# Two buffers for the gated output, two banks for the first final block's turns, two logits moved ahead

## The chip, the core and the metric

One core of a Trainium2 chip runs the whole program. The metric is the time of one execution on the device in microseconds; lower is better. TensorE (PE) multiplies, VectorE (DVE), ScalarE (ACT) and GpSimd (POOL) work element by element, and SyncE (SP) issues the DMAs. Each engine takes its instructions in the order of its own queue, and semaphores hold an instruction back until what it needs is there. Matmul results go to PSUM, eight banks of 128 x 512 float32.

## The reference

The input x is 2048 tokens of 512 features. Three layers follow one another:

```python
x = x + 0.5 * ffn(layernorm(x))
x = x + attn(layernorm(x))
x = x + 0.5 * ffn(layernorm(x))
```

`ffn` computes 64 router logits for each token, a softmax, keeps the 8 largest weights, and returns `flat * w_sum + w_dense @ expert_bias`. `attn` is a chunked linear attention with 32 heads (8 groups of 4) of 128 features and chunks of 128 tokens:

```python
scores = q_chunk @ k_chunk.T
decay = where(causal, exp(G[i] - G[j]), 0)
y = (scores * decay) @ xc + (q_chunk * exp(G)) @ prev_state
state = state * chunk_decay + k_dec.T @ xc
y = y / rms(y) * gnorm_w * silu(gate)
out = y.reshape(L, H * D) @ Wo.T
```

## The kernel before

x stays in SBUF as ACC, 16 chunks of 128 tokens. The first expert layer runs in four blocks of four chunks (f = 0 to 3). Then the attention runs over 8 groups g of heads, and in each over 16 steps n, one chunk each; the last expert layer runs in blocks f = 4 to 7 (NB = 4, so NB is the first final block). Products that need float32 accuracy are three bfloat16 products of high and low parts (`mm3`, L323 to L325).

A step n does the following, with the engine in brackets. `scores(n+1)` (PE, bank 2). `read_state(n)` (PE) multiplies the queries with the state into B_IN, bank 5. `attend(n)` (PE) multiplies PH, PL with the values into B_PV, bank 4, and then makes the chunk's state in bank 6; its first part waits for `gated(n-1)`, which reads B_PV. `scale_inter(n)` (DVE, L1649) writes B_IN times a decay to YF, `combine(n)` (DVE, L1656) adds YF into B_PV, `square(n)` (ACT, L1199) writes the squares to YF and their sums to SS, `inv_rms(n)` (POOL, L1453 RM, L1456 RR) takes the inverse root, `gated(n)` (DVE, L1689) writes B_PV times RR times the gate to YF. In the next step `z_hi(n)` (ACT, L1207) and `z_lo(n)` (POOL, L1449) split YF into ZS, a DMA turns it into ZT (`turn_z`), and two steps later `project_out(n)` (PE) multiplies it with Wo and `add_out(n)` (DVE, L1703) adds the product to ACC. Beside these, `decayed(n+1)` (DVE, L1640) waits for the scores, `p_hi(n+1)` (ACT, L1175) and `p_lo(n+1)` (POOL, L1445) split it into PH and PL, which `attend(n)` must have read, `mask_rows(n+2)` (POOL, L1423) prepares the next decay, `update_state(n)` (DVE, L1670), `state_hi(n)` (ACT, L1189) and `state_lo(n)` (DVE, L1678) carry the state on.

The order on each engine is written out by hand, in one `step` function for each engine: L1045 (PE), L1296 (ACT), L1519 (POOL) and L1799 (DVE). In the last group the final expert blocks are woven in. `pe_turn(NB, ...)` transposes chunks of ACC into a bank (L526), and `act_turned` copies the bank to XT (L536). Before, all four turns of block NB go to bank 0, so each waits for the copy of the one before it; the turns 1 and 3 stand between `scores` and `read_state` in the steps 13 and 14, the turns 0 and 2 at the ends of the steps 12 and 13. `pe_logits` (L553) multiplies XT with the router. `dve_logits`, `dve_choose` and `dve_weigh` pick the weights (L564 to L600), `pe_weights` (L617) transposes them, `pe_mix` (L645, L646) multiplies them with the expert biases, and `dve_mixed` (L701) adds the result to ACC. `pool_residual` (L670) scales ACC before.

`project_out` writes to bank 7 (B_OUT) up to n = 11 and to the banks 1 and 3 in turn from n = 12, in the last group. Behind the last step, PE's queue is `project_out(14)`, the weights and the mix of block NB, the logits of block NB + 1 (bank 7), a wait for the mix's last addition, `project_out(15)`, then the blocks NB + 1 to NB + 3. QF holds the rotated queries of a block of four chunks; in the last four steps there is no next block, so nothing is projected (`filled` is empty).

## Time and profile before

| | us |
|---|---|
| median of 3 runs | 1639.38 |
| lowest and highest | 1639.04, 1642.29 |
| profiled execution | 1642.75 |
| its span | 1640.9 |
| PE busy, share | 1589.4, 97% |
| POOL busy, share | 1411.7, 86% |
| DVE busy, share | 1368.9, 83% |
| ACT busy, share | 1093.0, 67% |

The trace is that of the profiled execution, and its times are microseconds from the start of the span. The span is what the core's instructions cover; 1.85 us of the profiled execution lie around it. A busy share is a mean over the whole span; what a change in one stretch is worth has to be read in that stretch. In a timeline row the bracket gives the idle time of the engine just before and what ended it. Operations of one engine overlap a little: the next one starts some 0.1 us before the end that is shown.

### The profile page before, as it was taken

The page shows a single profiled execution, that of the slowest core. Times are in us where ns is not written, and L with a number is a line of the kernel's source. Part 1 is how long each engine was busy: PE and PEld are TensorE (multiplying, and loading weights), DVE is VectorE, ACT ScalarE, POOL GpSimd, SP SyncE. Part 2 cuts the span into 40 slices and gives each one's busy share as a digit, 9 for nine tenths or more (in the row PEclk, how much of TensorE's full clock was granted, in tenths as well). Part 3 has the DMA queues.
Part 4 walks back from the last instruction along what each step waited for, and adds up shares of the span by engine and source line. Part 5 has one row for each costly group of instructions (what it writes and reads, how often), then busy time and mean ns, then how long its engine had stood idle before and what let it go on. Part 6 is the DMA issues. An engine that isn't in the chain of part 4 may idle for free.

```text
span 1640.9 us, 33589 instructions
## 1 busy us (share of the span) xinstructions
PE 1589.4 (97%) x11028; PEld 883.8 (54%) x11028; DVE 1368.9 (83%) x2945; ACT 1093.0 (67%) x2987; POOL 1411.7 (86%) x1316
## 2 busy tenths in 40 slices
PE   7898999999999999999999999999999999999986
PEld 5554555555555555555555555555555555555554
DVE  6988788888878888787878888788888878788876
ACT  4666677676766677766766667666776667666653
POOL 4767899888988899888998989888998889888974
PEclk8999999999999999999999999999999999999998
DMA  5123233232333223231332224323342224322222
GB/s 211 39 55 67 55 74 87 65 72 52 78 85 78 53 59 102 54 83 47 91 78 64 61 64 92 72 72 53 73 95 59 72 46 97 72 65 52 53 45 103
DMA packets 208012, 118.76 MB, mean 72 GB/s; under 512 B 173792, under 2 KB 174816, under 8 KB 206816
## 3 DMA queue, kind: packets, MB, share of 16 engines
q1 hardware_dynamic: 207840, 116.63, 29.7%
q8 instruction: 89, 1.46, 0.4%
q14 instruction: 83, 0.68, 0.1%
HBM read 70.19 MB, written 4.46 MB: 45 GB/s over the span
## 4 chain that ended last, share of the span: by engine, by line
PE 74%; POOL 11%; DVE 8%; issue 4%; ACT 2%; DMA 0%; ACTq 0%; POOLq 0%; DVEq 0%
PE B L325 23%; PE B L323 23%; PE B L324 23%; POOL QS L1410 2%; POOL ROWS L1423 2%; POOL RR L1456 1%; DVE WL L1696 1%; POOL PL L1445 1%; PE B L553 1%; POOL ZS L1449 1%; POOL WVF L1433 1%; POOL K L1417 1%; POOL WVL L1441 1%; POOL RM L1453 1%; DVE PF L1640 1%
## 5 line engine op out<-in xcount | busy, mean ns | idle before, releaser
L323 PE MATMUL B<-WH,XTH 128*128 128x128 bf16 (+1 forms) x992 | 269.3, 296 | 0.6 <-DVE QF L1610 0.6
L324 PE MATMUL B<-WL,XTH 128*128 128x128 bf16 (+1 forms) x992 | 269.3, 296 | 0.0
L325 PE MATMUL B<-WH,XTL 128*128 128x128 bf16 (+1 forms) x992 | 269.3, 296 | 0.0
L1410 POOL TENSOR_TENSOR QS<-QS,SIN 128x512 f32<-128x512 f32 x160 | 219.3, 1371 | 42.8 <-ACT QS L1137 42.7
L323 PE MATMUL B<-XTH,WH 128*128 128x512 bf16 x640 | 243.2, 380 | 1.0 <-DVE G L1630 1.0
L325 PE MATMUL B<-XTH,WL 128*128 128x512 bf16 x640 | 243.3, 380 | 0.0
L324 PE MATMUL B<-XTL,WH 128*128 128x512 bf16 x640 | 243.2, 380 | 0.0
L1689 DVE SCALAR_TENSOR_TENSOR YF<-B,RR,G 128x128 f32<-128x128 f32 x512 | 144.2, 344 | 113.4 <-POOL RR L1456 113.3
L1169 ACT ACTIVATE PF<-ROWS,NG 128x128 f32<-128x128 f32 x512 | 162.7, 389 | 79.1 <-POOL ROWS L1423 78.8
L1449 POOL TENSOR_TENSOR ZS<-YF,ZS 128x512 bf16<-128x512 f32 x128 | 158.0, 1235 | 64.5 <-ACT ZS L1207 64.2
L1136 ACT ACTIVATE QS<-B 64x512 f32<-64x512 f32 x160 | 94.9, 593 | 150.3 <-PE B L325 143.5
L1423 POOL TENSOR_TENSOR ROWS<-ROWS,AFTER 128x512 f32<-128x512 f32 x128 | 189.8, 1483 | 2.4 <-DMA ROWS<-rows_dram 2.4
L323 PE MATMUL B<-WH,ZT 128*128 128x512 bf16 x480 | 181.9, 379 | 0.2 <-DVE ACC L1703 0.2
L324 PE MATMUL B<-WL,ZT 128*128 128x512 bf16 x480 | 181.9, 379 | 0.0
L325 PE MATMUL B<-WH,ZT 128*128 128x512 bf16 x480 | 181.9, 379 | 0.0
L1678 DVE TENSOR_TENSOR STL<-ST,STH 128x512 bf16<-128x512 f32 x120 | 145.1, 1209 | 39.4 <-ACT STH L1189 37.6
L1445 POOL TENSOR_TENSOR PL<-PF,PH 128x512 bf16<-128x512 f32 x128 | 148.1, 1157 | 17.8 <-ACT PH L1175 17.4
L1640 DVE SCALAR_TENSOR_TENSOR PF<-B,DT,PF 128x128 f32<-128x128 f32 x512 | 143.0, 339 | 21.7 <-ACT PF L1169 20.2
L1199 ACT ACTIVATE YF<-B 128x128 f32<-128x128 f32 x512 | 134.0, 276 | 31.1 <-DVE B L1656 28.2
L1615 DVE TENSOR_TENSOR QF<-QF,QS 128x512 f32<-128x512 f32 x128 | 138.0, 1080 | 5.1 <-POOL QS L1410 4.0
L1433 POOL TENSOR_TENSOR WVF<-VF,WJ 128x512 f32<-128x512 f32 x120 | 141.8, 1181 | 0.2
L1456 POOL TENSOR_TENSOR RR<-RM,HALF 128x4 f32<-128x4 f32 x128 | 132.8, 1037 | 10.0
(209 smaller groups left out, 4320.9 us busy)
## 6 DMA issues: line engine op xcount, KB each, us to landing
ROWS<-rows_dram SPq DMA_DIRECT2D x128, 256.0 KB, 3.2
STAGE<-in_wall SPq DMA_DIRECT2D x108, 256.0 KB, 2.8
ACC<-in_x SPq DMA_DIRECT2D x3, 1024.0 KB, 10.0
out<-ACC SPq DMA_DIRECT2D x3, 1024.0 KB, 3.9
ZT<-ZS SPq DMA_TRANSPOSE x128, 3.1
ACC<-in_x SPq DMA_DIRECT2D x4, 256.0 KB, 3.6
COS<-in_cos SPq DMA_DIRECT2D x1, 1024.0 KB, 12.0
SIN<-in_sin SPq DMA_DIRECT2D x1, 1024.0 KB, 14.7
```

The costliest lines, as they stand in the source:

```text
L323: nc.tensor.matmul(out_, ah, bh, start=first, stop=False)
L324: nc.tensor.matmul(out_, ah, bl, start=False, stop=False)
L325: return nc.tensor.matmul(out_, al, bh, start=False, stop=last)
L1169: ins = nc.scalar.activation(PF[:, c], ROWS[:, n % 2, c], ACT.Exp, bias=tab(NG, g, n)[:, h:h + 1], scale=-1.0)
L1410: nc.gpsimd.tensor_tensor(QS[:, sl, :], QS[:, sl, :], SIN[:, t0:t0 + TB], ALU.mult).then_inc(sin_ready.sem, 1)
L1423: nc.gpsimd.tensor_tensor(rows, rows, AFTER[:, None, :].broadcast_to([P, G, P]), ALU.add).then_inc(rows_masked.sem, 1)
L1433: nc.gpsimd.tensor_tensor(WVF[:, :, :], VF[b % 2][:, None, s * P:(s + 1) * P].broadcast_to([P, G, P]), tab(WJ, g, n)[:, :, None].broadcast ...
L1445: nc.gpsimd.tensor_tensor(PL[:, :], PF[:, :], PH[:, :], ALU.subtract).then_inc(pl_ready.sem, 1)
L1449: nc.gpsimd.tensor_tensor(ZS[:, 1, :], YF[:, :], ZS[:, 0, :], ALU.subtract).then_inc(zl_ready.sem, 1)
L1456: nc.gpsimd.tensor_tensor(RR[:, :], RM[:, :], HALF[:, :], ALU.pow).then_inc(rr_ready.sem, 1)
L1640: ins = nc.vector.scalar_tensor_tensor(PF[:, c], B_S[:, c], dt[:, h:h + 1], PF[:, c], ALU.mult, ALU.mult)
L1678: nc.vector.tensor_tensor(STL[:, :], ST[:, :], STH[:, :], ALU.subtract).then_inc(stl_ready.sem, 1)
```

## The change

In the steps 13, 14 and 15 of the last group (`at_end`), the gated output and what becomes it lies in QF[:, 0, :] where n is odd and in YF where n is even (`y_of`). `scale_inter(n)` waits there for the `z_lo` of step n - 2 and, once, for the last readers of QF.

The turns of block NB go to the banks 0 and 7 in turn. The turns 0 and 1 have their banks free without a copy, but turn 1 waits for `add_out(10)`, the last reader of bank 7; turn 2 and turn 3 wait for the copies of the turns 0 and 1. Turn 1 moves behind `read_state(13)`, ahead of `attend(13)`; ScalarE's copy of it moves behind `wv_hi(14)`. `project_out(11)` writes to bank 3.

Behind the last step the logits of block NB + 1 are taken in two halves: chunks 0 and 1 ahead of the expert weights' turn of block NB, chunks 2 and 3 between that turn and the mix. Before, all four stood behind the mix.

```diff
--- before.py
+++ after.py
@@ -190,7 +190,7 @@
         def turned(f, i):
             if f < NB:
                 return t_bank("turn", f, i)
-            return BANK[0] if f == NB else BANK[(2, 6)[i % 2]]
+            return BANK[(0, 7)[i % 2]] if f == NB else BANK[(2, 6)[i % 2]]
 
         def t_bank(kind, f, i):
             return BANK[T_BANK[T_ORDER.index((kind, f, i)) % 3]]
@@ -329,7 +329,15 @@
             return BANK[EARLY_BANK[at]] if at < NFILL else RING[(at - NFILL) % len(RING)]
 
         def out_bank(n, last):
-            return RING[n % 2] if last and n >= NCH - BLK else B_OUT
+            return RING[n % 2] if last and n > NCH - BLK - 2 else B_OUT
+
+        def at_end(g, n):
+
+            return g == KVH - 1 and n > NCH - BLK
+
+        def y_of(g, n):
+
+            return QF[:, 0, :] if at_end(g, n) and n % 2 else YF[:, :]
 
         def tab(T, g, n):
 
@@ -516,8 +524,10 @@
                     pe.wait_ge(out_free.sem, out_free.at(KVH - 1, (f - NB) * BLK + i))
                 if f < NB:
                     t_free(pe, "turn", f, i)
+                elif f == NB and i >= 2:
+                    pe.wait_ge(f_xnt.sem, f_xnt.at(NB, i - 2))
                 elif f == NB and i:
-                    pe.wait_ge(f_xnt.sem, f_xnt.at(NB, i - 1))
+                    pe.wait_ge(out_free.sem, out_free.at(KVH - 1, NCH - BLK - 2))
                 elif f == NB + 1 and i < 2:
                     pe.wait_ge(st_ready.sem, st_ready.at(KVH - 1, cs_event(NCH - 2)))
                 elif f > NB:
@@ -940,7 +950,7 @@
 
 
                 into = out_bank(n, last)
-                if last and n >= NCH - BLK:
+                if last and n > NCH - BLK - 2:
                     pe.wait_ge(ring_free.sem, ring_free.at(g, use_of(NB - 1, NFILL - 1)))
                     pe.wait_ge(out_free.sem, out_free.at(g, n - 2))
                 else:
@@ -1050,13 +1060,15 @@
                         fill(g, b + 1, filled(n, last)[x], n, b == NB - 1, g + 1)
                 if not (last and n == NCH - 1):
                     scores(g, n + 1)
-                if last and n in (NCH - 3, NCH - 2):
-                    pe_turn(pe, NB, (1 if n == NCH - 3 else 3,))
+                if last and n == NCH - 2:
+                    pe_turn(pe, NB, (3,))
                 slot("A")
                 if g == 0 and n in SUMS_STEP:
                     pe.wait_ge(out_free.sem, out_free.at(0, n - 3))
                     pe_sums(pe, SUMS_STEP[n])
                 read_state(g, n)
+                if last and n == NCH - 3:
+                    pe_turn(pe, NB, (1,))
                 if last and n == NCH - 1:
                     pe_turn(pe, NB + 1, (0, 1))
                 if g == 0 and n == 0:
@@ -1090,9 +1102,10 @@
             for n in steps(True):
                 step(KVH - 1, n, True)
             project_out(KVH - 1, NCH - 2, True)
+            pe_logits(pe, NB + 1, (0, 1))
             pe_weights(pe, NB)
+            pe_logits(pe, NB + 1, (2, 3))
             pe_mix(pe, NB)
-            pe_logits(pe, NB + 1)
             pe.wait_ge(f_acc.sem, acc_at(NB, BLK - 1))
             project_out(KVH - 1, NCH - 1, True)
             pe_turn(pe, NB + 2)
@@ -1196,7 +1209,7 @@
                     act.wait_ge(zl_ready.sem, zl_ready.at(g, n - 1))
                 act.wait_ge(rm_ready.sem, rm_ready.at(g, n - 1))
                 for h in range(G):
-                    ins = nc.scalar.activation(YF[:, h * P:(h + 1) * P], B_PV[:, h * P:(h + 1) * P], ACT.Square,
+                    ins = nc.scalar.activation(y_of(g, n)[:, h * P:(h + 1) * P], B_PV[:, h * P:(h + 1) * P], ACT.Square,
                                                scale=float(P) ** -0.5, accum_out=SS[:, h:h + 1])
                 ins.then_inc(ss_ready.sem, 1)
 
@@ -1204,7 +1217,7 @@
                 act.wait_ge(z_ready.sem, z_ready.at(g, n))
                 if n or g:
                     act.wait_ge(z_turned.sem, 16 * z_turned.at(g, n - 1))
-                nc.scalar.activation(ZS[:, 0, :], YF[:, :], ACT.Copy).then_inc(zh_ready.sem, 1)
+                nc.scalar.activation(ZS[:, 0, :], y_of(g, n), ACT.Copy).then_inc(zh_ready.sem, 1)
 
             def both(i):
                 split_hi(0, i)
@@ -1327,8 +1340,6 @@
                     hi(g, b + 1, back["B"])
                 if g == 0 and n in SUMS_STEP:
                     act_sums(act, SUMS_STEP[n])
-                if last and n == NCH - 3:
-                    act_turned(act, NB, (1,))
                 if last and n == NCH - 2:
                     act_turned(act, NB, (3,))
                 if last and n == NCH - 1:
@@ -1348,6 +1359,8 @@
                 state_hi(g, n)
                 if nxt and ending:
                     wv_hi(g, n + 1)
+                if last and n == NCH - 3:
+                    act_turned(act, NB, (1,))
                 if n % NCH != 2:
                     next_weights()
                 if s >= 2 and now:
@@ -1446,7 +1459,7 @@
 
             def z_lo(g, n):
                 pool.wait_ge(zh_ready.sem, zh_ready.at(g, n))
-                nc.gpsimd.tensor_tensor(ZS[:, 1, :], YF[:, :], ZS[:, 0, :], ALU.subtract).then_inc(zl_ready.sem, 1)
+                nc.gpsimd.tensor_tensor(ZS[:, 1, :], y_of(g, n), ZS[:, 0, :], ALU.subtract).then_inc(zl_ready.sem, 1)
 
             def inv_rms(g, n):
                 pool.wait_ge(ss_ready.sem, ss_ready.at(g, n))
@@ -1645,15 +1658,18 @@
                 if n % NCH == 0:
                     return
                 dve.wait_ge(inter_full.sem, inter_full.at(g, in_event(n)))
-                dve.wait_ge(zl_ready.sem, zl_ready.at(g, n - 1))
-                nc.vector.tensor_tensor(YF[:, :].rearrange("p (h e) -> p h e", h=G), B_IN[:, :].rearrange("p (h e) -> p h e", h=G),
+                dve.wait_ge(zl_ready.sem, zl_ready.at(g, n - 2 if at_end(g, n) else n - 1))
+                if at_end(g, n) and n == NCH - 3:
+                    dve.wait_ge(qh_ready.sem, qh_ready.at(g, 5 * (NB - 1) + 1))
+                    dve.wait_ge(ql2_ready.sem, ql2_ready.at(g, 2 * (NB - 1)))
+                nc.vector.tensor_tensor(y_of(g, n).rearrange("p (h e) -> p h e", h=G), B_IN[:, :].rearrange("p (h e) -> p h e", h=G),
                                             tab(EG, g, n)[:, :, None].broadcast_to([P, G, P]), ALU.mult).then_inc(inter_read.sem, 1)
             def combine(g, n):
                 if n % NCH == 0:
                     return
                 dve.wait_ge(inter_read.sem, inter_read.at(g, in_event(n)))
                 dve.wait_ge(intra_full.sem, intra_full.at(g, n))
-                nc.vector.tensor_tensor(B_PV[:, :], B_PV[:, :], YF[:, :], ALU.add).then_inc(y_ready.sem, 1)
+                nc.vector.tensor_tensor(B_PV[:, :], B_PV[:, :], y_of(g, n), ALU.add).then_inc(y_ready.sem, 1)
 
             def update_state(g, n):
                 if n % NCH == NCH - 1:
@@ -1686,7 +1702,7 @@
                     dve.wait_ge(ring_free.sem, ring_free.at(g, use_of(b, NFILL - 1)))
                 for h in range(G):
                     c = slice(h * P, (h + 1) * P)
-                    ins = nc.vector.scalar_tensor_tensor(YF[:, c], B_PV[:, c], RR[:, h:h + 1], G2[:, s + b % 2 * (s == BLK - 1), c],
+                    ins = nc.vector.scalar_tensor_tensor(y_of(g, n)[:, c], B_PV[:, c], RR[:, h:h + 1], G2[:, s + b % 2 * (s == BLK - 1), c],
                                                          ALU.mult, ALU.mult)
                 ins.then_inc(z_ready.sem, 1)
```

## Rows read from the trace of the kernel before

**Rows 1.** Stage: length, busy PE, PEld, DVE, ACT, POOL, granted clock, DMA share, GB/s.

```profile
100.00:1400.00 1300.00, 1285.55 (x8809) 698.44 (x8810) 1089.41 (x2231) 888.54 (x2438) 1163.65 (x1015) 1.00 0.31 71
```

**Rows 2.** Timeline of DVE, steps 13 to 15: start, length, line, operation [idle].

```profile
1570.16 1.13 DVE L1689 SCALAR_TENSOR_TENSOR YF<-B,RR,G 128x128 f32<-128x128 f32 x4 [0.91 <-POOL RR L1456]
...
1572.24 0.67 DVE L1703 TENSOR_TENSOR ACC<-ACC,B 128x512 f32<-128x512 f32 x1
...
1573.29 0.69 DVE L1649 TENSOR_TENSOR YF<-B,EG 128x512 f32<-128x512 f32 x1 [0.38 <-POOL ZS L1449]
...
1574.02 0.70 DVE L1656 TENSOR_TENSOR B<-B,YF 128x512 f32<-128x512 f32 x1
...
1576.44 0.69 DVE L1678 TENSOR_TENSOR STL<-ST,STH 128x512 bf16<-128x512 f32 x1 [0.70 <-ACT STH L1189]
...
1578.32 1.13 DVE L1689 SCALAR_TENSOR_TENSOR YF<-B,RR,G 128x128 f32<-128x128 f32 x4 [1.19 <-POOL RR L1456]
...
1589.50 0.69 DVE L1649 TENSOR_TENSOR YF<-B,EG 128x512 f32<-128x512 f32 x1 [2.33 <-POOL ZS L1449]
...
1590.29 0.70 DVE L1656 TENSOR_TENSOR B<-B,YF 128x512 f32<-128x512 f32 x1
```

**Rows 3.** Timeline of PE, steps 13 to 15.

```profile
1570.83 0.63 PE L526 MATMUL B<-IDF,ACC 128*128 128x128 f32 x4 [1.43 <-ACT TXT L536]
...
1580.37 0.22 PE L323 MATMUL B<-VH,PH 128*128 128x128 bf16 x1
...
1589.35 0.22 PE L323 MATMUL B<-VH,PH 128*128 128x128 bf16 x1
...
1590.02 0.38 PE L323 MATMUL B<-WH,ZT 128*128 128x512 bf16 x1
```

**Rows 4.** Timelines of ACT and then POOL, step 13.

```profile
1572.90 0.63 ACT L1175 ACTIVATE PH<-PF 128x512 bf16<-128x512 f32 x1 [0.46 <-PE B L325]
...
1574.14 1.16 POOL L1445 TENSOR_TENSOR PL<-PF,PH 128x512 bf16<-128x512 f32 x1
...
1575.25 1.29 POOL L1423 TENSOR_TENSOR ROWS<-ROWS,AFTER 128x512 f32<-128x512 f32 x1
...
1576.48 0.71 POOL L1453 TENSOR_TENSOR RM<-SS,EPSC 128x4 f32<-128x4 f32 x1
...
1577.27 1.02 POOL L1456 TENSOR_TENSOR RR<-RM,HALF 128x4 f32<-128x4 f32 x1
```

**Rows 5.** Timelines of DVE and then POOL, an earlier step.

```profile
1442.53 1.76 DVE L1678 TENSOR_TENSOR STL<-ST,STH 128x512 bf16<-128x512 f32 x1
...
1442.02 1.72 POOL L1423 TENSOR_TENSOR ROWS<-ROWS,AFTER 128x512 f32<-128x512 f32 x1
```

**Rows 6.** Short stages as in rows 1; the clock stands before DMA share and GB/s.

```profile
1575.60:1579.00 3.40, 1.52 (x10) 0.76 (x7) 1.51 (x5) 3.40 (x11) 3.32 (x4) 1.00 0.03 5
...
1596.10:1599.50 3.40, 0.53 (x5) 0.23 (x4) 2.76 (x7) 2.12 (x7) 1.82 (x7) 1.00 0.41 77
...
1599.50:1602.90 3.40, 3.38 (x8) 1.37 (x9) 1.69 (x3) 0.00 (x0) 2.79 (x4) 0.50 0.02 5
```

**Rows 7.** Timelines of PE and DVE behind step 15, then the chain that ended last.

```profile
1598.43 0.40 PE L617 MATMUL B<-IDB,TWHL 128*128 128x128 bf16 x4 [2.20 <-DVE TWHL L600]
...
1599.52 0.61 PE L645 MATMUL B<-TEBH,TWT 128*128 128x512 bf16 x1 [0.69 <-ACT TWT L622]
...
1599.92 0.63 PE L646 MATMUL B<-TEBL,TWT 128*128 128x512 bf16 x1
...
1610.63 1.11 PE L526 MATMUL B<-IDF,ACC 128*128 128x128 f32 x8 [0.57 <-ACT TXT L536]
...
1606.84 0.83 DVE L564 SCALAR_TENSOR_TENSOR TLG<-B,RSTD,RB 128x64 f32<-128x64 f32 x4
...
1602.72 1.41 DVE L701 SCALAR_TENSOR_TENSOR ACC<-B,THRC,ACC 128x512 f32<-128x512 f32 x2 [0.45 <-POOL ACC L670]
...
1611.97 3.57 PE B L553 x32
```

## The prediction

> **What bounds the kernel now.** I read the table by stages first. In the long middle the reader sees TensorE busy 1285.55 of 1300 us at a granted clock of 1.00 [rows 1]: nothing that the change touches can matter there, and the change leaves it alone. All its edits lie in steps 13 to 15 of the last group and in the ten microseconds behind them, 1568 to 1611 us of the span. So the timelines of that stretch come next, engine by engine, and the question at each edit is which wait ends last. In step 13 VectorE idles 0.38 us before `scale_inter` (L1649), in step 15 it idles 2.33 us, both put down to GpSimd's `z_lo`, which still reads YF [rows 2]. TensorE idles 1.43 us before the second turn, for the copy out of bank 0 [rows 3]. From step 14's attend at 1580.37 (L323 on PH) to the end of `project_out(14)` it runs on through step 15's attend at 1589.35 and `project_out(13)` at 1590.02 [rows 3]. Then it idles 2.20 us before the expert weights' turn, 0.69 us more before the mix, and does the mix at half pace [rows 7].
>
> **Part 1, two buffers for the gated output.** Nothing is added to what is computed; `scale_inter` in steps 13 to 15 waits for a `z_lo` one step older. In step 13 it can follow `add_out(10)`: 1572.24 + 0.60 = 1572.84 for 1573.29, 0.45 us earlier. In step 15 the 2.33 us go. What is late next is `combine`, which also needs attend's product. In step 15 the twelve products start at 1589.35; twelve by 0.056 us (0.67) and the last one's 0.22 less 0.06 end them at 1590.18, and `combine` started at 1590.29 [rows 2, 3], 0.11 us behind. It was waiting for TensorE as much as for YF. So in step 15 the second buffer is worth 0.0 us unless TensorE comes earlier. The two new waits on QF's readers ended long before (the last projection block is over by then): 0.
>
> **Part 2, the turns in banks 0 and 7.** The second turn no longer waits for a copy but for bank 7, last read by `add_out(10)`, and stands between `read_state(13)` and `attend(13)`. `read_state(13)` can go right behind `scores(14)`, which ended at 1570.83 - 1.43 = 1569.40 [rows 3]: it runs from about 1569.3 to 1569.97, before the turn and not behind it. Now the wait: `add_out(10)` runs at 1572.24 for 0.67 us, behind `gated(12)` at 1570.16 and `decayed(14)`; none of these moves [rows 2]. The turn therefore starts at 1572.95, not 1570.83 (0.47 us to the next start), and `attend(13)`, queued behind it, at 1573.42, not 1571.97: **+1.45**. Its products end at 1574.25, and `combine(13)` starts at 1574.36 for 1574.02, +0.34 [rows 2]: more than Part 1 gave.
> Behind attend stand others. ScalarE's `p_hi(14)` waits for it: 1572.90 becomes 1574.35 (+1.45) [rows 4]. GpSimd's `p_lo(14)` was not bound by that (it started at 1574.14, behind GpSimd's own work), so it moves by 0.92 only, to 1575.06, and `mask_rows(15)` from 1575.25 to 1576.17, ending 1577.45 [rows 4]. VectorE's `state_lo(13)` moves from 1576.44 to 1576.78 [rows 2], into the middle of that operation. At 1442 us the trace has this meeting: `state_lo` began 0.51 us into `mask_rows` and took 1.76 us for 0.69, ending 0.55 us behind it [rows 2, 5]. So here it ends at about 1578.0, and GpSimd's RM, which starts during it, ends 0.1 us later, as now (1576.48, 0.71 us). `RR` starts at 1577.27 + 0.92 and `gated(13)`, 1.05 us behind RR's start, at 1579.24 for 1578.32: **+0.92**. If the two did not hold each other, RM would take 0.20 us, the rest of its shift would be saved, and the sum here would be +0.40.
> The Trainium skill ("SBUF — State Buffer", on the shared port pair) says that a VectorE operation with two SBUF inputs and a GpSimd one that reads SBUF exclude each other for a whole instruction, whichever starts first. It speaks against this change; rows 5 agree. By it this step costs +0.92, without it +0.40.
>
> **Part 3, step 14.** The fourth turn has its bank free, and TensorE's idle time before it goes. `scores(15)` and it come at +1.45, `read_state(14)` is over before 1579.7. `attend(14)` then waits for `gated(13)`: 1579.24 + 1.13 + 0.03 = 1580.40, for 1580.37 [rows 3]: **+0.03**. (Without the hold -0.45.) From there to `project_out(14)` TensorE has no gap, so step 15 keeps this shift. `project_out(11)` into another bank waits for nothing new: 0. Between 0 and +0.1 is my bound for all bank moves behind 1580.
>
> **Part 4, the clock.** The move opens a gap on TensorE: 1569.97 to 1572.95, 2.98 us in one piece, where it now idles 1.43. Behind the idle times of 2.20 and 0.69 us around the expert weights' turn (0.53 us busy from 1596.10 to 1599.50) the granted clock stood at 0.50 until 1602.90, that is 1.2 for 2.4 GHz; behind the 2.11 us of idle time that Part 3 removes (1.52 us busy from 1575.60 to 1579.00) it did not fall [rows 6, 7]. The new gap is the longest of these and I expect a fall. At the lower level the mix's 512-column products start 0.40 us apart and more [rows 7], each 0.61 or 0.63 long for 0.38 [rows 3]. The turn's 0.47 and attend's 0.67 us then take twice as long, **+1.1** for attend(13); everything of Part 2 hangs behind it, so `attend(14)` moves by 1.1 as well. Bounds: 0 (no fall) and 1.7 (3.4 us, as long as the low stretch of rows 6, at half pace and all on the path). I take 1.1.
> The Trainium skill ("TensorE: Matmul & The Clock Gate", Part 1) says that what watches the engine's activity runs on its own and doesn't start with the kernel. No single profile here can show that; by it some executions would fall in the gap and some not, which argues for a wide range and not for another sum.
>
> **Part 5, the second block's logits.** All 32 products take 3.57 us [rows 7], 16 take 1.79. The first half stands in the 2.20 us of idle time before the expert weights' turn: 0. The second half stands between that turn (1598.43, 0.22 us to the next) and the mix, which starts at 1600.44 for 1599.52, +0.92; the copy of the weights is ready in between. But with the gaps filled the clock should stay up, and a pair takes 0.43 us for 0.85. The four additions on VectorE (0.67 us apart, 0.75 long) start 0.70 us behind the mix's first product (0.21 to the second, its 0.38, and 0.11 as at `combine`) and end at 1600.44 + 0.70 + 2.01 + 0.75 = 1603.90, for 1602.72 + 1.41 = 1604.13 [rows 7]: **-0.23**. Bounds: at half pace +0.85; at best -0.9. Next the four statistics, then the logits' step at 1606.84. There VectorE shows no idle time [rows 7], so logits ready 6 us sooner give nothing. `project_out(15)` comes 2.4 us earlier; nobody on the path waits for it. The next block's last two turns follow ScalarE's copies, behind the exponentials, behind VectorE: they move with it.
> Sum: +0.03 + 1.1 - 0.23 = **+0.9 us** on the profiled execution, a span of 1641.8 us for 1640.9, 1643.7 us with what lies around it. The median of the three runs, 1639.38, is 3.37 us under the profiled 1642.75; from it, **1640.3 us**.
>
> **Rivals.** (a) No fall of the clock in the gap: 1639.2 us with the hold of Part 2, 1638.7 without. For it: 2.11 us of idle time left the clock alone, and 2.98 is not far from it. (b) The other side: the clock falls in more than one place. The early `project_out(15)` leaves TensorE idle from some 1607.6 to 1610.5, where it now waits 0.57 us [rows 7]. Behind that stand two blocks' logits, all on the path, so 3.4 us at half pace cost 1.3 to 1.7 us: 1641.8 us. If the mix stays at half pace too (+1.0), 1642.8. It decides once the clock falls behind both gaps of 2.9 us in one execution; the row of the 2.11 us shows that a gap does not always meet a fall, so both is the less likely. (c) The steps really come free: if `attend(13)` does not wait as I read it, step 13 gains 0.45 us and step 15 up to 2.33, 1636.6 us, or 1636.1 with the half microsecond of the mix. Against it: step 15's combine waits for TensorE already. (d) The logits' half costs what it seems, +0.9 on the mix because the mix runs at half pace all the same, +0.85 for -0.23: 1641.4.
>
> **How the numbers follow.** Forecast 0.45, (a) 0.24, (b) 0.15, (c) 0.06, (d) 0.10. About 0.2%, 3.3 us, is what a measurement of this kernel can tell from no change. The forecast, (a), (d) and nearly all of (b) lie within it; faster by more gets 0.04 from (c), slower by more 0.06 from (b) and a fall in a place that I did not see. The range goes from (a) without the hold, 1638.7, to (b), 1641.8, widened by half a microsecond on either side since the three runs scatter by 0.34 below and 2.91 above their median: 1638.1 to 1642.4.
>
> **What would show it.** In the timeline after: the second turn waits for L1703 and starts at about 1572.9; `attend(13)` stands behind it; `state_lo(13)` takes over 1 us; the 2.33 us wait of step 15 is gone but `combine(15)` is not earlier; the clock table shows a fall near 1572 and none at 1599.5; TensorE idles about 2.9 us near 1609. Wrong would be: `attend(13)` before 1573, or step 15's `combine` more than 1 us earlier.

## The result and the profile after

The changed kernel took 1642.82 us in the median of 20 executions (1639.23 to 1649.25), the kernel before 1640.97 in the median of 20 (1639.04 to 1643.82). The ratio is 1.002, with a 95% interval of 1.0011 to 1.003: slower by 0.1 to 0.3%. The medians are 1.85 us apart, the means 3.35 us (1644.70 and 1641.35), since the upper executions below weigh more in a mean. The forecast was 1640.3 in a range up to 1642.4.

The executions of the changed kernel stand in two groups: 12 from 1639.23 to 1643.14 and 8 from 1646.87 to 1649.25. The mean granted clock on record for each is 0.989 to 0.992 in the lower group and 0.986 to 0.987 in the upper, so the upper ones spent more time at the low clock. The kernel before has none above 1643.82 among these 20; in the 112 executions of it that were taken beside the experiments there are two (1646.48 and 1648.65), so such an execution is rare there, not impossible. The profiled execution, 1649.10 us, is one of the upper group. The head of its page:

```profile
span 1647.2 us, 33591 instructions
...
PE 1595.6 (97%) x11028; PEld 889.8 (54%) x11028; DVE 1368.2 (83%) x2945; ACT 1093.8 (66%) x2987; POOL 1412.4 (86%) x1316
```

The span is 6.3 us longer than that of before. TensorE is busy 6.2 us longer with the same 11028 products: they ran slower, not more of them.

The timeline of VectorE in the steps 13 to 15, which answers to [rows 2] (start, length, line, operation, idle time before; L1665 is `scale_inter`, L1672 `combine`, L1694 `state_lo`, L1705 `gated`):

```profile
1570.45 1.13 DVE L1705 SCALAR_TENSOR_TENSOR YF<-B,RR,G 128x128 f32<-128x128 f32 x4 [0.91 <-POOL RR L1469]
...
1572.53 0.68 DVE L1719 TENSOR_TENSOR ACC<-ACC,B 128x512 f32<-128x512 f32 x1
...
1573.12 0.68 DVE L1665 TENSOR_TENSOR QF<-B,EG 128x512 f32<-128x512 f32 x1
...
1575.83 0.70 DVE L1672 TENSOR_TENSOR B<-B,QF 128x512 f32<-128x512 f32 x1 [2.02 <-PE B L325]
...
1578.86 0.74 DVE L1694 TENSOR_TENSOR STL<-ST,STH 128x512 bf16<-128x512 f32 x1 [0.69 <-ACT STH L1202]
...
1580.51 1.13 DVE L1705 SCALAR_TENSOR_TENSOR QF<-B,RR,G 128x128 f32<-128x128 f32 x4 [0.91 <-POOL RR L1469]
...
1591.10 0.69 DVE L1665 TENSOR_TENSOR QF<-B,EG 128x512 f32<-128x512 f32 x1 [2.20 <-PE B L325]
...
1592.72 0.70 DVE L1672 TENSOR_TENSOR B<-B,QF 128x512 f32<-128x512 f32 x1 [0.93 <-PE B L325]
```

`scale_inter(13)` stands right behind `add_out(10)` (L1719), and the waits for GpSimd's `z_lo` are gone. In their place `combine(13)` waits 2.02 us for TensorE, and step 15 waits 2.20 and 0.93 us for it. From `gated(12)` to `combine(15)` it takes 1592.72 - 1570.45 = 22.27 us, for 1590.29 - 1570.16 = 20.13 in [rows 2].

TensorE's timeline at the second turn of the first final block, and at the last two turns of the third (answers to [rows 3] and [rows 7]):

```profile
1573.35 1.09 PE L536 MATMUL B<-IDF,ACC 128*128 128x128 f32 x4 [2.84 <-DVE ACC L1719]
...
1612.83 1.49 PE L536 MATMUL B<-IDF,ACC 128*128 128x128 f32 x8 [2.78 <-ACT TXT L546]
```

Both gaps of the prediction are there: 2.84 us that end with `add_out(10)`, the early gap, and 2.78 us where before idled 0.57, the late gap. The table by stages, cut where the granted clock changed (length, busy time of PE, PEld, DVE, ACT, POOL, clock, DMA share, GB/s):

```profile
1569.00:1572.40 3.40, 1.52 (x16) 0.78 (x13) 2.49 (x9) 2.61 (x7) 2.59 (x3) 1.00 0.01 3
1572.40:1575.80 3.40, 2.45 (x17) 2.28 (x18) 1.41 (x3) 0.00 (x0) 2.07 (x2) 0.51 0.36 67
1575.80:1579.20 3.40, 3.40 (x9) 1.21 (x8) 2.17 (x6) 2.78 (x11) 2.60 (x4) 0.50 0.05 10
...
1610.00:1613.40 3.40, 0.62 (x6) 0.54 (x6) 3.06 (x19) 2.40 (x10) 1.21 (x3) 1.00 0.00 0
1613.40:1616.80 3.40, 3.40 (x20) 3.34 (x20) 3.37 (x8) 1.68 (x3) 3.12 (x7) 0.50 0.00 0
...
1620.20:1623.60 3.40, 3.40 (x17) 3.10 (x17) 1.92 (x13) 0.88 (x2) 0.00 (x0) 0.50 0.00 0
```

The clock fell to 0.50 at both gaps: at the end of the first (1572.4) until 1579.2, 6.8 us, and behind the second (1613.4) until 1623.6, 10.2 us, with TensorE busy all the time in the latter. What the second one cost is read off VectorE's rows where the second and the fourth final block's logits are taken up (L574):

```profile
1609.07 0.83 DVE L574 SCALAR_TENSOR_TENSOR TLG<-B,RSTD,RB 128x64 f32<-128x64 f32 x4
...
1628.24 0.86 DVE L574 SCALAR_TENSOR_TENSOR TLG<-B,RSTD,RB 128x64 f32<-128x64 f32 x4 [1.57 <-PE B L563]
```

1628.24 - 1609.07 = 19.17 us. In the kernel before the stretch began at 1606.84 [rows 7] and ended at the start of this row of its trace:

```profile
1621.44 0.86 DVE L564 SCALAR_TENSOR_TENSOR TLG<-B,RSTD,RB 128x64 f32<-128x64 f32 x4 [1.24 <-PE B L553]
```

That is 14.60 us, so the second fall cost 4.57 us.

### The profile page after: what moved, and what is told of

Its sections match the earlier page's. It is cut to its first block, busy times and chain, and to the rows that moved or that the text cites. A ratio compares the mean times of both kernels' runs of the same rounds, so it can differ in the third digit from the quotient of the medians.

```text
span 1647.2 us, 33591 instructions
## 1 busy us (share of the span) xinstructions
PE 1595.6 (97%) x11028; PEld 889.8 (54%) x11028; DVE 1368.2 (83%) x2945; ACT 1093.8 (66%) x2987; POOL 1412.4 (86%) x1316
## 4 chain that ended last, share of the span: by engine, by line
PE 75%; POOL 11%; DVE 8%; issue 4%; ACT 2%; DMA 1%; ACTq 0%; POOLq 0%; DVEq 0%
PE B L323 23%; PE B L325 23%; PE B L324 23%; POOL QS L1423 2%; POOL ROWS L1436 2%; POOL RR L1469 1%; PE B L563 1%; DVE WL L1712 1%; POOL PL L1458 1%; POOL ZS L1462 1%; POOL WVF L1446 1%; POOL K L1430 1%; POOL RM L1466 1%; POOL WVL L1454 1%; DMA STAGE<-in_wall 1%
## 5 line engine op out<-in xcount | busy, mean ns | idle before, releaser
L1705 DVE SCALAR_TENSOR_TENSOR YF<-B,RR,G 128x128 f32<-128x128 f32 x504 | 141.9, 344 | 112.3 <-POOL RR L1469 112.3
L1694 DVE TENSOR_TENSOR STL<-ST,STH 128x512 bf16<-128x512 f32 x120 | 145.0, 1209 | 39.6 <-ACT STH L1202 37.8
```

Source lines behind the costliest of these rows:

```text
L1694: nc.vector.tensor_tensor(STL[:, :], ST[:, :], STH[:, :], ALU.subtract).then_inc(stl_ready.sem, 1)
```

## The experiments

A profile shows one execution, and between the profiles `gated(12)` starts anywhere from 1566.40 to 1571.28 us, so I compare intervals inside a profile. Three of them carry the argument: **A**, from `gated(12)` to `combine(15)`; **B**, from there to the second block's logits on VectorE; **C**, from there to the fourth block's. Beside them stand the late gap in the profile and, of all executions of the kernel, those above 1645 us.

| kernel | A | B | C | late gap | above 1645 |
|---|---|---|---|---|---|
| before | 20.13 | 16.55 | 14.60 | 0.57 | 2 of 132 |
| changed | 22.27 | 16.35 | 19.17 | 2.78 | 8 of 20 |
| e1: logits in halves only | 20.13 | 16.34 | 14.58 | 2.78 | 8 of 12 |
| e2: changed, logits in one piece | 21.04 | 16.38 | 14.60 | 0.38 | 0 of 12 |
| e3: changed, late gap filled | 20.24 | 16.35 | 14.61 | 0.66 | 0 of 12 |
| e4: changed, both gaps filled | 20.23 | 16.33 | 14.60 | 0.66 | 0 of 12 |
| e5: e3 with the turn behind attend | 19.20 | 16.33 | 14.59 | 0.65 | 0 of 11 |
| e10: e2 with the turn behind attend | 19.21 | 16.36 | 14.60 | 0.38 | 1 of 12 |
| e6: two buffers only | 19.88 | 15.51 | 14.59 | 1.19 | 0 of 11 |
| e7: before, filled ahead of the weights' turn | 21.76 | 15.50 | 14.60 | 1.19 | 0 of 12 |
| e8: all gaps filled | 19.21 | 15.51 | 14.59 | 0.65 | 0 of 11 |
| e12: all gaps filled, half ahead of the mix | 19.21 | 16.33 | 14.60 | 0.65 | 0 of 11 |
| e11: half behind the mix, late gap open | 19.21 | 15.52 | 19.00 | 2.80 | 0 of 11 |
| e9: `project_out(15)` behind the turns | 20.13 | 16.34 | 19.85 | 5.33 | 6 of 8 |

In the profiles of before, e2 and e10 the clock fell at the mix, in the others not; that is in B. e9 is a test of its own, with more work moved onto the path.

### The logits alone (e1_split_only)

```diff
             project_out(KVH - 1, NCH - 2, True)
+            pe_logits(pe, NB + 1, (0, 1))
             pe_weights(pe, NB)
+            pe_logits(pe, NB + 1, (2, 3))
             pe_mix(pe, NB)
-            pe_logits(pe, NB + 1)
```

Expected: 

> The kernel before, with the second block's logits in two halves around the expert weights' turn and nothing else of the change. Theory C (clock): project_out(15) comes earlier, TensorE then idles some 2.8 us ahead of the next block's last two turns, and in some executions the granted clock falls there and stays low through the logits; these lie 5 to 6 us above the kernel before, the others within 1 us of it, so the times stand in two groups and the median is -0.5 to +1 us unless the upper group holds more than half. Theory O (order): what costs is the place of the logits' second half ahead of the mix and of the turn ahead of attend, not the clock; then all executions lie +0.5 to +1 us above the kernel before, in one group, and no stretch of the trace behind 1605 us is at half clock that is not so before.

Measured: median 1645.56 us against 1641.65 (35 executions of before), ratio 1.0019 (1.0007 to 1.003). Eight of twelve executions lie between 1645.14 and 1648.22, and one of the 35 of before lies above 1645. The profiled one is of the lower group:

```profile
1611.52 1.11 PE L526 MATMUL B<-IDF,ACC 128*128 128x128 f32 x8 [2.78 <-ACT TXT L536]
...
1607.75 0.83 DVE L564 SCALAR_TENSOR_TENSOR TLG<-B,RSTD,RB 128x64 f32<-128x64 f32 x4
...
1622.33 0.86 DVE L564 SCALAR_TENSOR_TENSOR TLG<-B,RSTD,RB 128x64 f32<-128x64 f32 x4 [1.24 <-PE B L553]
```

The gap of 2.78 us is there, but in this execution the clock did not fall behind it, and interval C is 14.58 us, that of before. So the gap alone costs nothing and the upper group comes from this edit. That the clock fell in those eight is not seen in a profile. It is inferred from their mean clocks, 0.987 to 0.989 for 0.990 to 0.993 in the other four, and from the profiles that follow. Theory O expected one group. The median came out 3.9 us up; theory C had allowed for that only if the upper group held more than half, which it does.

### The change without it (e2_no_split)

```diff
-            pe_logits(pe, NB + 1, (0, 1))
             pe_weights(pe, NB)
-            pe_logits(pe, NB + 1, (2, 3))
             pe_mix(pe, NB)
+            pe_logits(pe, NB + 1)
```

Expected: 

> The changed kernel with the logits back in one piece behind the mix; the two buffers and the two banks stay. Theory C: no gap ahead of the next block's turns, so no group of executions 6 us up; the early gap stays and with it the fall near 1572 us in many executions: median +1 to +2.5 us over the kernel before. Theory O: only attend(13) behind the turn's wait costs, and most of it is hidden: 0 to +0.5 us, in one group.

Measured: 1640.59 us, ratio 0.9993 (0.9983 to 1.0003), highest 1644.08. The upper group is gone. The cost of 1 to 2.5 us that theory C expected did not show. The profile has the early fall, a short one:

```profile
1568.31 1.13 DVE L1704 SCALAR_TENSOR_TENSOR YF<-B,RR,G 128x128 f32<-128x128 f32 x4 [0.91 <-POOL RR L1468]
...
1589.35 0.70 DVE L1671 TENSOR_TENSOR B<-B,QF 128x512 f32<-128x512 f32 x1 [0.93 <-PE B L325]
...
1571.80:1575.20 3.40, 3.18 (x18) 1.97 (x17) 1.52 (x5) 1.78 (x9) 1.86 (x3) 0.50 0.41 77
```

A is 21.04 us, 0.91 over before, for a fall of 3.4 us. In the twelve executions together it did not count. That not all of them meet the fall would explain it, but no run shows it.

### Filling the late gap (e3_fill_late), and both (e4_fill_both)

```diff
+        def pe_fill(pe, into, count):
+            n = into.shape[-1]
+            for _ in range(count):
+                nc.tensor.matmul(into, WH[:, 0, 0:P], WH[:, 0, 0:n], start=True, stop=True)
...
-            pe_turn(pe, NB + 2)
+            pe_turn(pe, NB + 2, (0, 1))
+            pe_fill(pe, BANK[5][:, :], 10)
+            pe_turn(pe, NB + 2, (2, 3))
```

and in the second run also

```diff
                 if last and n == NCH - 3:
+                    pe_fill(pe, BANK[3][:, :], 11)
                     pe_turn(pe, NB, (1,))
```

Expected: 

> The changed kernel plus ten 512-column products into a free bank (2.2 us at full clock) between the two pairs of turns of the third final block, where TensorE idles 2.78 us. Nobody reads them. Theory C: the clock no longer falls at about 1613 us, the executions near 1649 are gone, and the median is that of the changed kernel's lower group less 0 to 1 us: 1641 to 1642.5, -0.2 to +1.5 us against the kernel before. Theory O: work added changes nothing or costs up to 1 us; the upper group stays (about a third of the executions near 1649).

Expected of both: 

> As the run before, and eleven 512-column products (2.4 us) ahead of the turn that waits for add_out(10) in step 13, where TensorE idles 2.84 us. Theory C: no fall near 1572 us either; what is left is the shift by the wait itself. Median -1 to 0 us against the kernel before, in one group. Theory O: as the changed kernel, +1 to +2 us.

Measured: 1641.41 us, ratio 1.0 (0.999 to 1.0009), highest 1644.68; and 1640.56, ratio 0.9998 (0.9989 to 1.0006), highest 1643.53. Work that nobody reads took the upper group away, here and in e5, e8 and e12: none of these 57 executions lies above 1645. This is the direct test of theory C: order and waits are those of the changed kernel, only the gap is smaller (0.66 us for 2.78). The profile of the first, TensorE, VectorE and GpSimd:

```profile
1570.72 0.63 PE L541 MATMUL B<-IDF,ACC 128*128 128x128 f32 x4 [2.84 <-DVE ACC L1726]
...
1608.22 1.11 PE L541 MATMUL B<-IDF,ACC 128*128 128x128 f32 x8 [0.66 <-ACT TXT L551]
...
1567.83 1.13 DVE L1712 SCALAR_TENSOR_TENSOR YF<-B,RR,G 128x128 f32<-128x128 f32 x4 [0.91 <-POOL RR L1476]
...
1574.56 1.21 DVE L1701 TENSOR_TENSOR STL<-ST,STH 128x512 bf16<-128x512 f32 x1 [0.71 <-ACT STH L1209]
...
1588.07 0.70 DVE L1679 TENSOR_TENSOR B<-B,QF 128x512 f32<-128x512 f32 x1 [0.93 <-PE B L325]
...
1573.94 1.28 POOL L1443 TENSOR_TENSOR ROWS<-ROWS,AFTER 128x512 f32<-128x512 f32 x1
```

The first gap is as long as in the changed kernel and no fall came behind it in this execution, so it shows what the order alone costs in the steps: A is 1588.07 - 1567.83 = 20.24 us, 0.11 over before. `state_lo` (L1701) began 0.62 us into `mask_rows` (L1443) and took 1.21 us for 0.69, as Part 2 expected. In the changed kernel's own profile, where the clock fell, it took 0.74 us and met nothing: there `mask_rows` came later too.

### The turn behind attend (e5_behind_attend, e10_no_split_behind)

```diff
                 read_state(g, n)
-                if last and n == NCH - 3:
-                    pe_turn(pe, NB, (1,))
...
                 attend(g, n)
+                if last and n == NCH - 3:
+                    pe_turn(pe, NB, (1,))
```

The first of the two has the filled late gap too; the second has the logits in one piece and nothing filled.

Expected: 

> The changed kernel with the ten products in the late gap, and the second turn behind attend(13) in place of ahead of it. Theory Q (queue): what the two buffers could give was lost because attend(13) stood behind the turn's wait for add_out(10). Then attend(13) starts at gated(12)'s end, some 2 us sooner than in the changed kernel, attend(14) and all behind it 0.9 us sooner than in the kernel before; median -0.5 to -1.5 us against the kernel before and no fall of the clock near 1572 us. Theory P (paced elsewhere): steps 13 to 15 are paced by GpSimd and VectorE anyway, so the place of the turn changes nothing: within 0.3 us of the kernel with the late filler alone (ratio 1.000).

Expected of the second: 

> The changed kernel with the logits back behind the mix and the second turn behind attend(13); no products added. By theories C and Q: no late gap, no early gap, attend(14) 0.9 us sooner than in the kernel before; -0.5 to -1.5 us in the median and no execution above 1645 that the kernel before has not too. If the gain of the run with the turn behind attend came from the added products or from the logits' first half, 0 to -0.3 us.

Measured: 1639.14 us against 1641.58, ratio 0.9989 (0.9981 to 0.9998); and 1641.57 against 1641.89, ratio 0.9995 (0.9986 to 1.0004). The second's profile, TensorE's attend(13) and VectorE:

```profile
1571.33 0.23 PE L323 MATMUL B<-VH,PH 128*128 128x128 bf16 x1 [1.12 <-DVE YF L1704]
...
1570.15 1.13 DVE L1704 SCALAR_TENSOR_TENSOR YF<-B,RR,G 128x128 f32<-128x128 f32 x4 [0.91 <-POOL RR L1468]
...
1589.36 0.70 DVE L1671 TENSOR_TENSOR B<-B,QF 128x512 f32<-128x512 f32 x1 [0.93 <-PE B L325]
...
1605.72 0.86 DVE L574 SCALAR_TENSOR_TENSOR TLG<-B,RSTD,RB 128x64 f32<-128x64 f32 x4 [0.49 <-PE B L563]
```

`attend(13)` starts 0.05 us behind `gated(12)`'s end. A is 19.21 us, 0.92 less than before, where 0.9 was expected. The second block's logits now wait 0.49 us for TensorE, yet B is 16.36 for 16.55, so nothing of the 0.92 is lost up to there. The executions do not show it: the median is 0.32 us lower where 0.5 to 1.5 was expected, which is as near to the rival's 0 to 0.3, and one execution, 1645.23, lies above all of before in that set (1643.39). Theory Q holds in the profile. A gain in time over before is shown only together with the filled gap (e5), and how much of that gain is the turn's place is not shown.

### Two buffers alone (e6_two_buffers_only)

```diff
-                dve.wait_ge(zl_ready.sem, zl_ready.at(g, n - 1))
+                dve.wait_ge(zl_ready.sem, zl_ready.at(g, n - 2 if at_end(g, n) else n - 1))
...
```

with `y_of` for YF as in the change.

Expected: 

> The kernel before with the two buffers for the gated output and nothing else. By the prediction's Part 1: scale_inter of step 15 comes 1 to 2 us sooner and combine(15) does not, 0 us; step 13's combine comes up to 0.45 us sooner and is given back at state_lo against mask_rows. 0 to -0.4 us in all, in one group. If YF was what paced the steps, -1.5 to -2.5 us.

Measured: 1640.29 us, ratio 0.9993 (0.9984 to 1.0002).

```profile
1567.41 1.13 DVE L1700 SCALAR_TENSOR_TENSOR YF<-B,RR,G 128x128 f32<-128x128 f32 x4 [0.91 <-POOL RR L1464]
...
1573.23 1.11 DVE L1689 TENSOR_TENSOR STL<-ST,STH 128x512 bf16<-128x512 f32 x1 [0.70 <-ACT STH L1197]
...
1585.67 0.69 DVE L1660 TENSOR_TENSOR QF<-B,EG 128x512 f32<-128x512 f32 x1 [1.77 <-PE B L325]
...
1587.29 0.70 DVE L1667 TENSOR_TENSOR B<-B,QF 128x512 f32<-128x512 f32 x1 [0.93 <-PE B L325]
```

A is 19.88 us, 0.25 less than before. Step 15's `scale_inter` waits for TensorE in place of `z_lo`, and `combine` 0.93 us more. `state_lo(13)` (L1689) took 1.11 us for 0.69, as expected. In this profile the clock did not fall at the mix, though nothing is filled, and B is 15.51 us for 16.55.

### The mix at full clock (e7_before_fill_mix)

```diff
             project_out(KVH - 1, NCH - 2, True)
+            pe_fill(pe, BANK[7][:, 256:512], 16)
             pe_weights(pe, NB)
```

Expected: 

> The kernel before plus sixteen 256-column products (1.8 us) where TensorE idles 2.20 us ahead of the expert weights' turn. Theory C: the mix behind it then runs at full clock in all executions; the additions end about 0.9 us sooner: -0.3 to -0.9 us in the median. Theory O: no gain, 0.

Measured: 1641.42 us, ratio 0.9996 (0.9985 to 1.0006): no gain that can be measured. Two stages and two rows of VectorE:

```profile
1576.20:1579.60 3.40, 1.29 (x8) 0.64 (x7) 1.60 (x5) 3.26 (x9) 3.32 (x4) 1.00 0.00 0
...
1579.60:1583.00 3.40, 3.39 (x28) 3.34 (x29) 2.54 (x7) 1.23 (x2) 1.35 (x2) 0.51 0.03 7
...
1592.30 0.70 DVE L1662 TENSOR_TENSOR B<-B,YF 128x512 f32<-128x512 f32 x1 [0.93 <-PE B L325]
...
1607.80 0.82 DVE L569 SCALAR_TENSOR_TENSOR TLG<-B,RSTD,RB 128x64 f32<-128x64 f32 x4
```

B is 15.50 us, 1.05 less than before, so the mix at full clock was worth more than expected in this execution. The median is 0.16 us lower, short of theory C's 0.3 to 0.9. In an execution where the clock doesn't fall at the mix anyway, as in the profile of e6, nothing is to be gained; how many of before's are such is not on record. The stages show another thing: here the clock fell in step 14, behind a gap of 2.11 us that is in the kernel before too and behind which its profile shows no fall [rows 6]. A is 21.76 us here, 1.63 more than before, and the gain in B was lost by it.

### All gaps filled (e8_all_gaps, e12_all_gaps_split)

The first is the kernel of e5 with these two edits, the second has the last one only:

```diff
             pe_weights(pe, NB)
-            pe_logits(pe, NB + 1, (2, 3))
             pe_mix(pe, NB)
+            pe_logits(pe, NB + 1, (2, 3))
...
             pe_weights(pe, NB + 2)
+            pe_fill(pe, BANK[2][:, :], 12)
             pe_mix(pe, NB + 2)
```

Expected: 

> The turn behind attend(13), two buffers, the logits' first half ahead of the expert weights' turn and the second behind the mix, the late filler, and twelve 512-column products ahead of the mix of the third final block, where TensorE idles 3.1 us. By theories C and Q together: -0.9 us from the steps, -0.9 from the mix, -0.5 to -1.3 from the third block's mix at full clock: -1.5 to -3 us, in one group. If only one of the two holds, -0.5 to -1.5.

Expected of the second: 

> The run with all gaps filled, but with the logits' second half ahead of the mix, as the change has it. By the prediction's Part 5 the half costs 0.9 us at the mix's start, of which the additions on VectorE hide a part, since they wait for GpSimd's scaled chunks at full clock: 0.5 to 0.9 us slower than the run with all gaps filled, -1 to -2 us against the kernel before. If the place of that half is free, the ratio is the same as there, 0.9985.

Measured: 1638.96 us against 1641.58, ratio 0.9985 (0.9977 to 0.9994), the lowest ratio of all, though its interval overlaps those of e5 and e12; and 1640.73 against 1641.47, ratio 0.9991 (0.9982 to 0.9999).

```profile
1589.84 0.70 DVE L1680 TENSOR_TENSOR B<-B,QF 128x512 f32<-128x512 f32 x1 [0.93 <-PE B L325]
...
1605.35 0.83 DVE L579 SCALAR_TENSOR_TENSOR TLG<-B,RSTD,RB 128x64 f32<-128x64 f32 x4
...
1619.94 0.86 DVE L579 SCALAR_TENSOR_TENSOR TLG<-B,RSTD,RB 128x64 f32<-128x64 f32 x4 [1.24 <-PE B L568]
```

A, B and C are 19.21, 15.51 and 14.59 us. With the half ahead of the mix B is 16.33: that half costs 0.82 us at full clock. The twelve products ahead of the third block's mix were expected to give 0.5 to 1.3 us; from the fourth block's logits to the end of the span it is 19.26 us for before's 19.46, 0.2 less.

### The half behind the mix, nothing filled (e11_half_behind_mix)

```diff
             pe_logits(pe, NB + 1, (0, 1))
             pe_weights(pe, NB)
-            pe_logits(pe, NB + 1, (2, 3))
             pe_mix(pe, NB)
+            pe_logits(pe, NB + 1, (2, 3))
```

and the turn behind attend.

Expected: 

> The changed kernel with the second turn behind attend(13) and the logits' second half behind the mix; no products added. Steps: -0.9 us as in the run with the late filler. The mix starts with its weights' copy and at full clock: -0.5 to -0.9 us. But project_out(15) still comes some 2 us sooner than before, so by theory C the late gap is 2 to 3 us and an upper group of executions, 4 to 6 us up, is back: median -1 us to +2 us, spread wide, highest above 1645. If instead the logits' half ahead of the mix was what made the gap costly, no upper group: -1 to -2 us and highest below 1644.

Measured: 1642.74 us against 1641.47, ratio 1.0003 (0.9993 to 1.0014). The profiled execution took 1644.89, one of four between 1644.47 and 1644.93:

```profile
1608.94 1.11 PE L536 MATMUL B<-IDF,ACC 128*128 128x128 f32 x8 [2.80 <-ACT TXT L546]
...
1605.15 0.83 DVE L574 SCALAR_TENSOR_TENSOR TLG<-B,RSTD,RB 128x64 f32<-128x64 f32 x4
...
1624.15 0.86 DVE L574 SCALAR_TENSOR_TENSOR TLG<-B,RSTD,RB 128x64 f32<-128x64 f32 x4 [1.89 <-PE B L563]
...
1610.00:1613.40 3.40, 3.40 (x21) 3.40 (x18) 3.12 (x9) 1.18 (x3) 3.21 (x7) 0.51 0.00 0
...
1616.80:1620.20 3.40, 3.40 (x17) 2.97 (x17) 2.83 (x18) 1.89 (x7) 0.00 (x0) 0.50 0.00 0
```

A and B are 1.95 us shorter than before, but the gap of 2.80 us and the fall behind it are back, and C is 19.00 us. The median is level with before, and the highest execution stayed just under the 1645 that was expected. This is the second profile of a fall behind the late gap, and it costs 4.40 us.

### What ends a fall (e9_products_first)

```diff
             pe.wait_ge(f_acc.sem, acc_at(NB, BLK - 1))
-            project_out(KVH - 1, NCH - 1, True)
             pe_turn(pe, NB + 2)
             pe_weights(pe, NB + 1)
+            project_out(KVH - 1, NCH - 1, True)
             pe_logits(pe, NB + 2)
```

on the kernel of e1.

Expected: 

> The kernel before with the logits in two halves, and project_out(15) moved from ahead of the third final block's turns to behind the second block's weights' turn, directly ahead of the third block's logits. The gap on TensorE becomes some 5.5 us, so the clock should fall in nearly every execution. Theory K (kind of work): in the changed kernel the clock stayed low for 10.2 us because what ran there were float32 logits and turns; with twelve 512-column bfloat16 products first it is back at 1.00 within 3.4 to 6.8 us, and the logits behind them take about 3.6 us for the 7.0 of the changed kernel. Theory L (length): a fall behind a long gap lasts some 10 us whatever runs; then the logits take 6 to 7 us here too. The time: the fall and 2.6 us of products come onto the path, +3 to +6 us over the kernel before by either.

Measured: 1646.78 us against 1641.89, ratio 1.0033 (1.0022 to 1.0043), in the range of both theories (3 to 6 us up).

```profile
1601.80:1605.20 3.40, 0.00 (x0) 0.00 (x0) 3.30 (x23) 0.62 (x4) 1.66 (x4) 0.54 0.48 195
...
1608.60:1612.00 3.40, 3.40 (x12) 1.41 (x11) 0.00 (x0) 1.08 (x2) 2.80 (x4) 0.50 0.00 0
...
1613.20:1616.60 3.40, 3.40 (x33) 3.40 (x32) 3.23 (x7) 0.00 (x0) 0.00 (x0) 1.00 0.00 0
```

The clock was low from 1601.8 to 1612.0 and back at 1.00 for the third block's logits, which took 3.7 us (from 1613.1 to 1616.8) and not 7.0. That is what theory K said of them. But the fall came while TensorE still idled, and it too lasted 10.2 us in all, as theory L has it. The run does not separate the two. For K stand the falls of 3.4 us in which bfloat16 products ran ([rows 6], e2) and those of 10.2 us with float32 logits. Against K as the whole answer stands the early fall of the changed kernel, 6.8 us with bfloat16 products. So does the start-up, which no edit touches: from 15.8 us on the clock was low for 10.2 us in the profile of before, and for 3.4 us in that of e5:

```profile
17.60:21.00 3.40, 3.02 (x13) 1.92 (x15) 3.00 (x9) 2.61 (x6) 3.23 (x8) 0.50 1.03 430
21.00:24.40 3.40, 3.40 (x29) 2.97 (x29) 3.36 (x6) 0.78 (x2) 3.32 (x6) 1.00 1.00 398
```

What decides the length stays open.

## Why the prediction was wrong, point by point

**The base.** It started from a median of three runs, 1639.38. Twenty executions gave 1640.97. Of the 2.5 us between forecast and measurement 1.6 are this; as a difference between the kernels 0.9 was forecast and 1.85 measured. In the four other sets of executions the kernel before had medians of 1641.47 to 1641.89, so part of even the 1.85 may be the set. The prediction had seen three times spread over 3.3 us and still took their median as known to half a microsecond.

**Part 1** (two buffers) said 0: alone they gave 0.25 us of A and no time that can be measured. Right.

**Part 2 and 3** (the turn ahead of attend) said +0.03 us at step 15: the profile with the gap and without a fall shows +0.11. The turn started behind `add_out(10)` as derived, the hold of `state_lo` by `mask_rows` showed (1.21 us), and with the turn behind attend A became 1.04 us shorter (e3 to e5). By the Trainium skill ("SBUF — State Buffer") the two exclude each other for a whole instruction, whichever starts first; the rows of e3 agree: `state_lo` ended 0.55 us behind `mask_rows`.

**Part 4** (the clock) is the step that failed, together with rival (b), in the price of a fall. Where the early fall comes was right: 1572.4. Its price was put at +1.1 us, the turn and attend at half pace, with 1.7 as the bound, from a low stretch as long as that of [rows 6]. In the changed kernel's profile the stretch was 6.8 us and A was 2.03 us longer than without a fall (22.27 for e3's 20.24); in e2's it was 3.4 us and A was 0.80 longer. The bound was a duration taken from one row. And this fall, the one in the sum, is not what moved the measurement: e2 and e3 keep the early gap and are level with before (0.9993 and 1.0).

**The late gap** had no term in the sum. Part 5 let `project_out(15)` come 2.4 us earlier and said that nobody on the path waits for it. Rival (b) did name the gap before the third block's last turns and found it to be 2.9 us (2.78 measured), gave it a chance of 0.15 for both falls together, and priced it at 1.3 to 1.7 us. By the two groups it came in 8 of 20 executions of the changed kernel, and cost 4.57 us in its profile and 4.40 in e11's. The same error: 3.4 us at half pace, where it was 10.2. e1 has this gap and no early one and is slower by its own; e3 closes it and is level with before. So the difference between the kernels comes from the late gap. The account leaves one thing open: the median of the twelve lower executions is 1642.5, above before's too, and no profile was taken of one of them.

A row of the profile before would have told that a low stretch can last longer. In the start-up, where float32 turns and logits run among bfloat16 products, it lasted as long:

```profile
15.80:19.20 3.40, 2.59 (x13) 1.48 (x12) 3.26 (x12) 1.61 (x4) 2.63 (x8) 0.50 1.02 417
...
22.60:26.00 3.40, 3.40 (x14) 2.38 (x15) 1.67 (x4) 0.00 (x0) 2.07 (x5) 0.51 0.80 301
```

Rival (b) was argued down with the 2.11 us gap of before, behind which the clock stayed up. What the profiles show is that the place of a fall is not set by the gap alone: e1 had the late gap of 2.78 us and no fall, e3 the early one of 2.84 and none, and e7 a fall in step 14 behind the very 2.11 us where before's profile has none. The Trainium skill ("TensorE: Matmul & The Clock Gate", Part 1) says that the monitor doesn't start with the kernel. These three pairs of profiles agree with that, and the prediction should have made the falls a matter of chance for each gap, with the price of each, and not a forecast of one.

**Part 5** (the logits) said -0.23 us for the mix and nothing for the logits themselves: B went from 16.55 to 16.35, -0.20. Right, and it hid two sizes of about one microsecond: the mix at full clock gave 1.05 (e7), the half ahead of it took 0.82 (e8 and e12). What it overlooked is the late gap, above.

**The sum for the profiled execution**: 0.3 us later at `gated(12)`, 2.14 in A, -0.20 in B, 4.57 in C make 6.8. The span is 6.3 us longer, so 0.5 came back behind the fourth block's logits.

## What to carry to other kernels

An edit that lets a queue run ahead opens a gap further on, and the gap can cost more than the wait that it removed: look at what TensorE does until its next work that is on the path, and fill it, or leave the work where it is. In a new gap take the clock's fall as a chance, and price it by the longest low stretch that the profile shows, not by the shortest. Where a wait stands in a queue ahead of work that others need, put it behind that work: here one moved turn shortened its stretch by 1.0 us (e3 to e5). And where executions scatter by 3 us, take the base from many of them.

## What the hardware showed that I had not expected

With TensorE busy for 10.2 us on float32 turns and logits, the granted clock stayed at 0.50 (1613.4 to 1623.6, and 1610.0 to 1620.2 in e11), and 32 logits products took 7.0 us for 3.6. Gaps of the same 2.8 us were followed by a fall in some profiles (the changed kernel, e2, e11) and by none in others (e1, e3). That executions of one kernel differ in this is inferred from their two groups and mean clocks.
